# Attention and mixture-of-experts layer on one Trainium2 core: SyncE stores Q and K of a half before it fetches either, and VectorE's parts, maximum and inverse change places

## The reference, cut to what matters

```
xn = layernorm(x)
q, k, v = split(xn @ w_qkv + b_qkv)             # 16 heads of 16
for each window n of 128 tokens, stride 64:
    o[n] = softmax(q[n] @ k[n].T / sqrt(16)) @ v[n]
attn = concat(o)[:, :512] @ w_out + b_out
y = sum over the best 2 experts e of p_e * (silu(xn @ w1_e) * (xn @ w2_e)) @ w3_e
out = x + attn + y
```

## Time and profile before

| | us |
|---|---|
| median of 3 runs (lowest to highest) | 801.11 (800.93 to 801.87) |
| the profiled execution, its own time | 801.99 |
| its span, first to last instruction | 799.8 |
| TensorE busy | 722.6 (90%) |
| VectorE busy | 581.6 (73%) |
| ScalarE busy | 417.4 (52%) |
| GpSimd busy | 319.7 (40%) |

### The profile page before, as it was taken

How to read it: one execution, slowest core, us unless ns; L and a number is a source line. 1 busy time by engine, 2 the same in 40 slices (tenths; PEclk the granted TensorE clock), 3 DMA queues, 4 the chain that set the end, 5 groups by cost and what they waited for, 6 DMA issues and landing times.

```text
span 799.8 us, 18229 instructions
## 1 busy us (share of the span) xinstructions
PE 722.6 (90%) x6144; PEld 580.0 (73%) x6145; DVE 581.6 (73%) x975; ACT 417.4 (52%) x769; POOL 319.7 (40%) x360
## 2 busy tenths in 40 slices
PE   0996887979999999999999999999979897979795
PEld 0975665857888788878787878887767676767674
DVE  5954899857777777777877777777648695959564
ACT  0221232346667666766677666766425464646443
POOL 4000398022445444454444444543102354545433
PEclk9986798888999999999999999999979999989898
DMA  8997174371111111111111111111355766764710
GB/s 270 317 314 199 41 207 152 102 246 51 46 52 46 52 46 52 53 46 46 52 48 50 46 52 52 48 49 41 101 166 171 190 204 165 224 174 142 230 57 28
DMA packets 66178, 92.61 MB, mean 116 GB/s; under 512 B 6256, under 2 KB 53232, under 8 KB 66128
## 3 DMA queue, kind: packets, MB, share of 16 engines
q1 hardware_dynamic: 56096, 65.68, 27.4%
q0 software_dynamic: 6864, 18.75, 7.4%
q10 hardware_dynamic: 3168, 7.48, 2.7%
HBM read 59.06 MB, written 32.83 MB: 115 GB/s over the span
## 4 chain that ended last, share of the span: by engine, by line
PE 67%; DMA 18%; DVE 7%; SPq 4%; issue 2%; ACT 1%; DVEq 0%; ACTq 0%; POOLq 0%; POOL 0%
PE PS L1151 60%; DMA parts_scratch<-WORK 11%; PE PS L1378 4%; DMA KS<-parts_scratch 3%; PE PS L1356 2%; SPq L371 2%; DVE SMALL L839 2%; SPq L387 2%; DMA XN<-in_x 1%; DVE XN L1016 1%; PE PS L1174 1%; DMA xt_scratch<-WALL 1%; DMA WORK<-xt_scratch 1%; DVE WALL L833 1%; DVE WORK L833 1%
## 5 line engine op out<-in xcount | busy, mean ns | idle before, releaser
L333 DVE TENSOR_TENSOR WS<-WALL,WS 128x1024 fp32r<-128x1024 f32 x144 | 176.5, 1226 | 86.7 <-ACT WS L765 82.5
L1151 PE MATMUL PS<-WS,XTS 128*128 128x512 f32 x852 | 234.5, 411 | 2.2 <-DVE XTS L833 1.5
L1151 PEld LDWEIGHTS PS<-WS,XTS 128*128 128x128 f32 x852 | 151.0, 190 | 46.3 <-DVE XTS L833 13.1
L765 ACT ACTIVATE WS<-WALL 128x1024 fp32r x144 | 152.2, 1058 | 38.2 <-issue 35.6
L1151 PE MATMUL PS<-WALL,WORK 128*128 x568 | 136.2, 383 | 0.8 <-ACT WORK L781 0.8
L707 ACT ACTIVATE WORK<-PS 128x512 f32<-128x512 f32 x128 | 70.1, 595 | 92.2 <-PE PS L1151 90.0
L1151 PEld LDWEIGHTS PS<-WALL,WORK 128*128 128x128 f32 x568 | 102.2, 190 | 13.0 <-issue 1.0
L616 POOL DMA_INDIRECT WORK<-xn_scratch,WORK x72 | 98.5, 1368 | 24.8 <-issue 21.6
L839 DVE TENSOR_REDUCE SMALL<-PS 128x8 f32<-128x1024 f32 x64 | 76.9, 1201 | 34.4 <-PE PS L1151 34.4
L620 POOL DMA_INDIRECT ys_scratch<-SIDE,WORK x36 | 41.6, 1156 | 115.3 <-ACT SIDE L791 115.3
L583 POOL TENSOR_TENSOR OTS<-SIDE,XN 128x256 f32<-128x256 f32 x32 | 23.9, 748 | 138.3 <-DVE XN L1016 137.0
(11 more groups left out here) (125 smaller groups left out, 1092.4 us busy)
## 6 DMA issues: line engine op xcount, KB each, us to landing
WALL<-ys_scratch SPq DMA_DIRECT2D x16, 512.0 KB, 6.6
parts_scratch<-WORK SPq DMA_DIRECT2D x32, 240.0 KB, 3.8
QS<-parts_scratch SPq DMA_DIRECT2D x16, 480.0 KB, 4.0
WALL<-in_wexp ACTq DMA_DIRECT2D x16, 384.0 KB, 5.7
WALL<-in_wexp SPq DMA_DIRECT2D x16, 384.0 KB, 6.2
XN<-in_x SPq DMA_DIRECT2D x4, 1024.0 KB, 12.9
xn_scratch<-XN SPq DMA_DIRECT2D x4, 1024.0 KB, 7.0
WALL<-in_x SPq DMA_DIRECT2D x8, 512.0 KB, 5.0
```

The source lines that it names most:

```text
L333: eng.tensor_tensor(out=WS[:, 1 - k, half, 1], in0=weights, in1=WS[:, 1 - k, half, 0].bitcast(F32), op=ALU.subtract).then_inc(low_ready[ha ...
L765: act.activation(WS[:, 1 - k, half, 0], weights, ACT.Copy).then_inc(high_ready[half], 1)
L1151: return pe.matmul(o, a, b, start=start, stop=stop)
```

## The change

It has two parts. On SyncE, `stacks` (but for its first call, whose order stays the same) stores both blocks of a half and then fetches both: store Q, store K, fetch Q, fetch K, for half 0, then for half 1; before, it was store Q, fetch Q, store K, fetch K for each half. On VectorE, `split_rest` and `split_parts` become one `split`, and a unit's order goes from turned maximum, inverse, rest, maximum, parts 1 and 2 to turned maximum, rest, parts 1 and 2, maximum, inverse. In sequence 7, which has no blocks to split, this leaves maximum ahead of inverse. No operation is added or taken away.

```diff
@@ stacks (SyncE)
-                for n, blk in enumerate(BLOCKS):
-                    sp.wait_ge(parts_ready, nb * 4 + n + 1)
-                    out_(blk)
-                    if not at_once:
-                        back(blk)
-                if at_once:
-                    store_xt(5)
-                    for blk in BLOCKS:
-                        back(blk)
+                for half in range(2):
+                    for n in (2 * half, 2 * half + 1):
+                        sp.wait_ge(parts_ready, nb * 4 + n + 1)
+                        out_(BLOCKS[n])
+                    if at_once and half:
+                        store_xt(5)
+                    if not at_once or half:
+                        for n in range(0 if at_once else 2 * half, 2 * half + 2):
+                            back(BLOCKS[n])
@@ split_rest and split_parts become split (VectorE)
-            def split_rest(n, first=False):
+            def split(n, first=False):
...
                 else:
                     rest.then_inc(w_free, 1)
-
-            def split_parts(n, first=False):
-
-                blk = BLOCKS[n]
-                if not first:
                     dve.wait_ge(w_free, c["W"].now() + 1)
                 link(dve.tensor_copy(PARTS[:, 1, blk, :], REST))
@@ batch (VectorE)
-                    if u in (2, 4, 6) or (u == 0 and pending):
-                        invert()
                     if b == EXTRA and u == 0:
                         dve.wait_ge(y_stored, 1)
                     if not last and u < 4:
-                        split_rest(u)
+                        split(u)
                     if not (last and u >= UNITS - 3):
                         take_max()
-                    if not last and u < 4:
-                        split_parts(u)
+                    if u in (2, 4, 6) or (u == 0 and pending):
+                        invert()
```

More of the change, by code:

```diff
@@ L946, in _ @@
             for n in range(4):
-                split_rest(n, True)
-                split_parts(n, True)
+                split(n, True)
             route(0)
```

## The result

The changed kernel takes 773.44 us (median of 4 runs, 772.02 to 774.76) against 801.49 before beside it; the ratio is 0.9646, 95% interval 0.962 to 0.9672. The forecast was 772, with a range of 765 to 786.

A forecast was written before the change was run, and what follows sets the result against it. It took K's store-fetch chain through SyncE to bound five sequences: stalls 20.6, clock 11.7, sequence 7 1.3, sequences 0 and 1 0.7, less VectorE 2.5 and overlap 2.5, gaining 29.3 from 801.99: 772.7, forecast 772, range 765 to 786.

The forecast's parts named there:

- The stalls, 20.6 us: TensorE's five waits in sequences 2 to 6 for K's parts from DRAM; all 20.6 us were to go.
- signs of being wrong: TensorE waiting over 0.5 us for L583 or L991, last K store over 5 us, clock below 1.00 after unit 6.
- SyncE's step: SyncE issues block 3's store 3.7 us late in sequence 5; the new order sends it directly behind block 2's.
- The overlap term: Two stores overlapping and Q's fetch starting later were to cost 0.5 us a sequence, 2.5 in all.
- the margin: Time by which the last fetch lands ahead of TensorE's arrival: 0.8 us in sequence 5, under 1.2 us everywhere.
- The clock, 11.7 us: TensorE's clock, granted at half or little more behind four of five stalls, was to give back 11.7 us.
- VectorE's pace: VectorE's new order costs TensorE 0.75 us per sequence in sequences 4 to 6, 2.5 us in all.
- The wait for part 0: In unit 0 VectorE waits 1.2 us with nothing to do for ScalarE's part 0.
- The subtraction beside GpSimd: VectorE's subtractions and GpSimd's reads exclude each other: perhaps 1 us more per sequence in sequences 4 to 6, 775.
- Sequences 0 and 1: Tokens for sequence 1 sooner against the inverse moved later: gain 0.7 us, bounds -1.7 and +3.
- Sequence 7: TensorE's two waits of 0.83 us for the maximum behind an inverse go: 1.66 us, counted as 1.3.
- 772.7: The whole sum: 29.3 us taken from the profiled execution's 801.99 us.

The follow-up runs named there:

- store_late: Kernel before, K's store of each half issued after Q's store landed but ahead of Q's fetch, VectorE's order as before: 772.14 us, ratio 0.9629.
- sp_q_first: Kernel before with SyncE's new order, except that Q's fetch is issued just before K's store in each half: 805.29 us, ratio 1.0056.
- dve_only: Kernel before with VectorE's new order alone, SyncE's order old: 786.32 us, ratio 0.9828.
- filled9: Kernel before with 9 idle products on TensorE in the place of the stall: 789.13 us against 801.70, ratio 0.9854.
- sp_only: Kernel before with SyncE's new order alone, VectorE's order old: 766.92 us, ratio 0.9585; repeated, 768.50 us.
- inv_first: Changed kernel with the inverse back behind the turned maximum, ahead of the split: 773.55 us, ratio to the kernel before 0.9634.

## Why the forecast came out, step by step

- **The stalls, 20.6 us, go: right**, and they left nothing behind, as the sum had it. None of its signs of being wrong came; the nearest was the wait for the turned maximum (L985), which reached 0.5 us.
- **SyncE's step: the right place, half of the reason.** The forecast said that the last store is 3.7 us late and that this lateness is the gain. The lateness is gone, 0.03 us in the changed kernel, but it is not all. The forecast missed that K's store stands behind Q's fetch in the queue of transfers and takes 2 us more for it, in both halves: `store_late`, which differs from `sp_q_first` by one swap, has the gain but for the last 4 to 5 us, with half of the lateness still there. The forecast's own reason holds too: in `dve_only` the stall follows the lateness, and in the two sequences where SyncE happened not to be late it was 0.2 us and none. That is one trace, so how the gain divides over the two reasons stays open; the change does both.
- **The overlap term, 5 x 0.5 us, was mis-sized with the wrong sign.** K's store took 2.0 us less than 4.3, and K's fetch 0.7 more than 3.5: the pair is 1.3 quicker, where 0.5 slower was forecast. The total hardly shows it, because once the stall is zero a still earlier fetch is worth nothing; it is why no sequence had a stall although the margin had been called thin.
- **The clock, 11.7 us: right in size.** TensorE's busy time in sequences 2 to 7 fell by 12.5, and `filled9` gave 12.6 by its median (801.70 to 789.13).
- **VectorE's pace: right in size, in part for another reason.** 0.75 us a sequence in sequences 4 to 6 was forecast; 34.9 against the 34.1 of `sp_only` is 0.8. The wait for part 0 measured 1.14 for 1.2. But the turned maximum, which was to carry the cost, made TensorE wait 0.5 us a sequence where it was 0.3; the rest is 0.2 for the maximum (L839), 0.1 in smaller gaps and 0.27 of busy time (34.07 against 33.80).
- **The subtraction beside GpSimd.** By the Trainium skill's rule (SBUF, State Buffer) on operations with two SBUF inputs beside a reading GpSimd operation, the forecast had estimated up to 1 us a sequence more. Of the three operations that were moved together only the subtraction has two full-size inputs there; the copy, which has one, varies too, from 0.33 to 0.83 us in the changed kernel. In the changed kernel the copies and subtractions took 0.3 us a sequence more, 4.9 for 4.6, so the 1 us did not come; in `inv_first` they took 1.7 more. The divide was not late for TensorE in sequences 2 to 6.
- **Sequences 0 and 1: a gain of 0.7 forecast, a loss of 1.8 measured**, just outside the bound of 1.7. The tokens did come sooner (the stall of 1.61 us is gone), and SyncE's part alone gains there: `sp_only` begins the second stage at 564.4, its repeat at 563.8, for 565.9 before. VectorE's part loses more: `dve_only` begins it at 568.6. The inverse moved behind the split, and the split had to wait for ScalarE's part 0, so in unit 2 of sequence 0 the inverse ran at 101.94 instead of 97.75. GpSimd, in its fixed order, waited with its divide until 103.84 instead of 99.63; two runs of sixteen operations of 0.7 us (L575, which make the places for the experts' rows) stand behind it, and the divide behind those came at 126.92 instead of 123.48, for which TensorE waited 2.42 us. `inv_first` gives 4.5 us back there. The forecast had looked at the divide only in the later stage, where GpSimd has gaps.
- **Sequence 7: 1.3 forecast, 2.1 measured.** The forecast's own term was right: the two waits of 0.83 are gone, and ScalarE's waits grew by 0.3, which leaves 1.4. The rest is TensorE's busy time, 25.31 for 26.15, at a granted clock of 0.95 for 0.90, which the forecast did not have.
- **That 772.7 and 772.46 agree so closely is luck.** The overlap term was 2.5 us too careful and sequences 0 and 1 were 2.5 us worse than forecast.
- **That the change's second part was not needed** the forecast did not say; it priced it as a small loss beside a large gain, and did not ask for the gain of SyncE's part alone, which is 5 us more.

What stays open: why K's store lands 2 us later behind Q's fetch; the runs show the order and the price, not what inside the transfer engines makes it. Open too is what makes the copies and subtractions longer when they stand together.

## What to carry to other kernels

Where one engine issues a store whose landing somebody waits for and a large fetch whose landing nobody wants yet, issue the store first: being behind the fetch cost 2 us a time (1.3 after what the next fetch gave back), in a chain that passed it twice a period. When a stall is found, count the clock behind it too; filling the stall with idle products measures that bill, here 12 of 28 us. And price each part of a change alone: here one part was 5 us better without the other.

## What the runs showed of the hardware that was not expected

The clock does not follow from the length of the stall. After a stall of 3.39 us in the kernel before it stayed at 1.00, in `dve_only` after one of 2.97 too; in the kernel with half 1's new order it fell after one of 2.20, and stayed low into the next unit. The kernel with half 0's new order has both within one trace: its five stalls were 2.20, 2.16, 2.81, 2.09 and 2.21 us, and the 4.5 us behind them ran at 0.62, 1.00, 0.62, 1.00 and 0.62. The stall of half 1's kernel, and the two stretches behind it:

```profile
590.01 0.62 PE L1155 MATMUL PS<-KS,QS 96*128 96x128 bf16 x8 [2.20 <-DMA KS<-parts_scratch]
```
```profile
590.00:594.50 4.50, 4.49 (x58) 3.69 (x59) 1.78 (x4) 1.17 (x2) 0.04 (x1) 0.62 0.89 281
594.50:598.50 4.00, 4.00 (x47) 2.99 (x47) 1.39 (x2) 0.03 (x1) 0.00 (x0) 0.58 0.31 88
```

TensorE had been busy for the whole 7.8 us up to that stall, at 1.00. The first stretch took 4.5 us for 58 instructions where 57 take 2.7 at 1.00, so a stall of 2 us can cost as much again or nothing. What decides between the two the runs do not show. And a product of 128x128 with 128x256 in float32 took 0.43 us at full clock when 14 stood in a row; my 0.27 was a misreading of the timeline, which counts each such product as two instructions.
